# A three-layer decoder block on one core: third buffers for two tiles, a 128x128 turn, and new orders on all five engines

## What is computed

```python
# layer 1: recurrent attention, 32 heads of 16, mixed with the row before
xx = shifted(x) - x
r, k, v, g = ((x + xx * maa_i) @ Wi.T + bi for each i)     # four projections
y = (r @ k * Wm) @ v                                        # decay and bonus in Wm
y = (head_norm(y) * ln_g + ln_b) * silu(g);  x = x + y @ Wo.T + bo
# layer 2: attention over ctx_512, 32 query heads, 8 key/value heads
x = x + softmax(q @ k / 4) @ v
# layer 3: MLP; inputs of both products are quantised in blocks of 32 to 8 bits
h = mx_linear(mx_layernorm(x), W1, b1);  h = mx_gelu(h)
x = x + bf16_round(residual + mx_linear(h, W2, b2))
```

## Time and profile before

| | |
|---|---|
| median of 3 runs | 1352.62 us |
| lowest and highest | 1351.16, 1355.15 us |
| span of the profiled execution, first to last instruction | 1347.5 us |
| PE busy | 1243.7 us, 92% |
| DVE busy | 1137.6 us, 84% |
| ACT busy | 797.9 us, 59% |
| POOL busy | 660.0 us, 49% |
| chain that ended last | PE 52%, DVE 20%, issue 10%, ACT 6%, POOL 6%, DMA 4% |

### The profile page before, as it was taken

One profiled execution on the slowest core, in us unless ns is written; L12 is line 12 of the kernel. 1 busy time (PEld: TensorE's weight loads), 2 busy tenths in 40 slices (PEclk: granted clock), 3 DMA queues, 4 the chain that ended last, 5 costly groups with the idle time before them and its releaser, 6 DMA issues.

```text
span 1347.5 us, 34631 instructions
## 1 busy us (share of the span) xinstructions
PE 1243.7 (92%) x13352; PEld 795.7 (59%) x13352; DVE 1137.6 (84%) x1960; ACT 797.9 (59%) x1565; POOL 660.0 (49%) x700
## 2 busy tenths in 40 slices
PE   4778999999999999999999999999999999999864
PEld 4556556666665556666555666655566666566421
DVE  7899888888888888888888888888888898889885
ACT  3334657566666675666667665566666665675541
POOL 6767354555454444544444454544445444445332
PEclk9889999999999999999999999999999999999987
DMA  7664332222233222122322212223122322222222
GB/s 240 165 152 118 83 81 54 55 60 57 63 67 70 71 49 54 52 62 67 71 71 49 55 51 59 71 70 70 38 53 60 65 71 70 51 59 57 60 57 51
DMA packets 137331, 97.09 MB, mean 72 GB/s; under 512 B 108112, under 2 KB 110160, under 8 KB 136400
## 3 DMA queue, kind: packets, MB, share of 16 engines
q1 hardware_dynamic: 137168, 94.87, 27.9%
HBM read 37.16 MB, written 8.39 MB: 34 GB/s over the span
## 4 chain that ended last, share of the span: by engine, by line
PE 52%; DVE 20%; issue 10%; ACT 6%; POOL 6%; DMA 4%; SPq 1%; ACTq 0%; POOLq 0%; DVEq 0%
PE bank_b L549 12%; PE bank_y L603 7%; PE bank_a L549 7%; PE bank_a L539 5%; PE rt L618 3%; PE rt L631 3%; PE rt L568 2%; DVE att L1430 2%; DVE negm L1459 2%; DVE amax_g L1500 2%; PE bank_a L658 2%; PE bank_o L595 2%; PE bank_b L658 2%; PE bank_o L637 2%; DMA xin<-x 2%
## 5 line engine op out<-in xcount | busy, mean ns | idle before, releaser
L3011 POOL TENSOR_TENSOR gmem<-gmem,unit_g 128x1024 bf16<-128x1024 bf16 x64 | 125.9, 1968 | 250.8 <-DVE unit_g L1512 250.8
L1459 DVE TENSOR_REDUCE negm<-rt 128x16 f32<-128x2048 f32 x64 | 145.9, 2280 | 3.1 <-PE rt L618 2.8
L2433 ACT ACTIVATE pT<-rt 128x2048 f32<-128x2048 f32 x64 | 119.9, 1873 | 23.3 <-PE rt L631 17.3
L667 PE MATMUL bank_y<-w2q,gmem 128*128 128x512 bf16 x512 | 120.6, 387 | 8.3 <-DMA gmem<-gmem 8.3
L549 PE MATMUL bank_a<-mix_r,w_Wr 128*128 128x128 f32 x1024 | 125.2, 282 | 0.9 <-POOL mix_r L2970 0.9
L549 PEld LDWEIGHTS bank_a<-mix_r,w_Wr 128*128 128x128 f32 x1024 | 120.5, 197 | 7.8 <-issue 7.7
L549 PEld LDWEIGHTS bank_b<-mix_k,w_Wk 128*128 128x128 f32 x1024 | 118.3, 193 | 5.2 <-issue 3.8
L549 PE MATMUL bank_b<-mix_g,w_Wg 128*128 128x128 f32 x1024 | 120.4, 276 | 1.1 <-POOL mix_g L2970 1.0
L549 PE MATMUL bank_b<-mix_k,w_Wk 128*128 128x128 f32 x1024 | 119.8, 275 | 1.3 <-DMA w_Wk<-Wk 1.2
L603 PE MATMUL bank_y<-w_Wo,yT 128*128 128x512 f32 x256 | 116.3, 597 | 3.7 <-issue 2.2
L549 PEld LDWEIGHTS bank_b<-mix_g,w_Wg 128*128 128x128 f32 x1024 | 116.8, 192 | 4.0 <-issue 3.2
(11 more groups left out here) (185 smaller groups left out, 2814.1 us busy)
## 6 DMA issues: line engine op xcount, KB each, us to landing
qx<-qdense SPq DMA_DIRECT2D x64, 224.0 KB, 3.0
context<-ctx SPq DMA_DIRECT2D x32, 384.0 KB, 3.2
gmem<-w SPq DMA_DIRECT2D x16, 512.0 KB, 4.1
xin<-x SPq DMA_DIRECT2D x32, 256.0 KB, 3.3
out<-x SPq DMA_DIRECT2D x32, 256.0 KB, 3.0
vp<-vz SPq DMA_DIRECT2D x32, 128.0 KB, 3.1
odense<-oT SPq DMA_DIRECT2D x128, 32.0 KB, 1.9
pT<-Wv SPq DMA_DIRECT2D x1, 1024.0 KB, 8.9
```

The costliest lines, as they stand in the source:

```text
L667: done = e.matmul(bank_y[:, :], gqT[:, t, :], w2q[:, t, :], start=(t == 0), stop=(t == FT - 1))
L1459: e.tensor_reduce(negm[:, 0:H].rearrange("p (g a j) -> p g j a", g=4, a=2)[:, :, 2 * i:2 * i + 2, :], rt[:, :].rearrange("p (g j a s) -> p ...
L2433: e.activation(pT[:, :, :].rearrange("p g n -> p (g n)"), rt[:, :], ACT.Exp, scale=float(D) ** -0.5).then_inc(sem(f"act_ex{i}"), 1)
L3011: e.tensor_tensor(blocks(half), blocks(half), per_block(unit[f"g{i}"], 32), ALU.mult).then_inc(sem(f"pool_gsc{i}"), 1)
```

## The change

xin and x2 get a third buffer each, and the semaphores that count their loads and stores become three. `next_x(n)` waits for `first_sum` of n - 3 rather than n - 2, and `normalise_o(n)` for the store of n - 3. oden becomes [128, 128], set to zero once on POOL, and `turn_sums` transposes all of it. Every other step computes what it did; each engine has the same steps as before, 866 on PE, 1414 on DVE, 1084 on ACT, 339 on POOL and 398 on SP, in another order. The loops are shorter: `range(13, 25)` on PE, `range(14, 24)` on DVE, `range(13, 25)` on ACT, `range(14, 25)` on POOL, `range(17, 24)` on SP; the turns around them are written out singly. Waits in the lists that an earlier wait already covers are left out.

```diff
-        xin = [sb(f"xin{i}", [P, C]) for i in range(2)]
+        xin = [sb(f"xin{i}", [P, C]) for i in range(3)]
...
-        oden = sb("oden", [H, T])
+        oden = sb("oden", [P, T])
...
-        x2 = [sb(f"x2_{i}", [P, C]) for i in range(2)]
+        x2 = [sb(f"x2_{i}", [P, C]) for i in range(3)]
...
             def next_x(n):
-                if n >= 2:
-                    e.wait_ge(sem("dve_x1"), n - 1)
-                    load_x(n)
+                if n >= 3:
+                    e.wait_ge(sem("dve_x1"), n - 2)
+                load_x(n)
...
             def turn_sums(n):
...
-                e.transpose(bank_o[:, 0:H], oden[:, :], ident[0:H, 0:H]).then_inc(sem("pe_dT"), 1)
+                e.transpose(bank_o[:, 0:P], oden[:, :], ident[:, :]).then_inc(sem("pe_dT"), 1)
...
             def normalise_o(n):
...
-                if n >= 2:
-                    e.wait_ge(sem(f"sp_out{n % 2}"), 16 * (n // 2))
+                if n >= 3:
+                    e.wait_ge(sem(f"sp_out{n % 3}"), 16 * (n // 3))
...
             load("masks")
+            load_w12(0)
             load("columns")
             load("heads")
-            load_w12(0)
             load_x(0)
             load_w12(1)
+            load("Wv")
+            load("Wk")
             load_x(1)
-            load("Wv")
             load("Wr")
```

More of the change, by code:

```diff
@@ L1793, in _ @@
             norm_mv("g", 2)
+            mixed(5, "k")
+            gate(4)
             weighted(2)
+            stats_q(6)
             hidden(2)
@@ L1923, in _ @@
             hidden(5)
-            mixed(8, "v")
+            gelu_max(4, 1)
             hidden_max(5)
@@ new lines, in _ @@
+            up_out(6, 0, bank_a)
+            first_sum(8)
+            stats_x(8)
+            gelu_max(6, 0)
+            gelu_pow2(6, 0)
+            norm_mv("x", 8)
+            decayed(9, 0)
+            up_out(6, 3, bank_b)
+            denominators(7)
+            second_out(5)
+            residual(5)
+            differences(10)
+            mixed(10, "v")
+            maxima(8, 1)
+            normalise_o(7)
+            gelu_round(6, 0)
+            up_out(6, 2, bank_a)
+            stats_f(7)
@@ new lines, in _ @@
+            mixed(10, "k")
+            maxima(8, 0)
+            gate(9)
+            norm_mv("f", 7)
+            decayed(9, 1)
+            stats_g(7)
+            norm_mv("g", 7)
+            gelu_max(6, 1)
+            weighted(7)
+            hidden(7)
+            hidden_max(7)
+            gelu_pow2(6, 1)
+            hidden_pow2(7)
+            hidden_scale(7)
+            gelu_quantised(6, 0)
+            hidden_round(7)
+            hidden_quantised(7)
+            scaled_y(9)
+            stats_q(11)
@@ new lines, in _ @@
+            maxima(9, 1)
+            up_out(7, 2, bank_a)
+            gelu_quantised(7, 0)
+            mixed(11, "v")
+            mixed(11, "k")
+            normalise_o(8)
+            residual(6)
+            maxima(9, 0)
+            stats_f(8)
+            norm_mv("f", 8)
+            gate(10)
+            decayed(10, 1)
+            stats_g(8)
+            norm_mv("g", 8)
+            weighted(8)
+            hidden(8)
+            hidden_max(8)
+            gelu_max(7, 1)
+            hidden_pow2(8)
@@ new lines, in _ @@
+            decayed(11, 0)
+            gelu_pow2(8, 0)
+            denominators(9)
+            second_out(7)
+            residual(7)
+            up_out(8, 2, bank_a)
+            differences(12)
+            normalise_o(9)
+            maxima(10, 1)
+            mixed(12, "v")
+            mixed(12, "k")
+            maxima(10, 0)
+            stats_f(9)
+            norm_mv("f", 9)
+            gelu_round(8, 0)
+            gelu_max(8, 1)
+            gate(11)
+            gelu_quantised(8, 0)
@@ new lines, in _ @@
+            stats_q(13)
+            norm_mv("q", 13)
+            first_sum(11)
+            stats_x(11)
+            norm_mv("x", 11)
+            decayed(12, 0)
+            gelu_max(9, 0)
+            gelu_pow2(9, 0)
+            up_out(9, 3, bank_b)
+            denominators(10)
+            differences(13)
+            maxima(11, 1)
+            normalise_o(10)
+            second_out(8)
+            up_out(9, 2, bank_a)
+            mixed(13, "v")
+            maxima(11, 0)
+            stats_f(10)
@@ L1966, in _ @@
[L1966 to L1976 removed]
+            decayed(22, 1)
+            stats_g(20)
+            norm_mv("g", 20)
+            weighted(20)
+            hidden(20)
@@ new lines, in _ @@
+            normalise_o(22)
+            up_out(21, 2, bank_a)
+            maxima(23, 1)
+            mixed(25, "v")
+            maxima(23, 0)
+            stats_f(22)
+            mixed(25, "k")
+            norm_mv("f", 22)
+            gelu_round(21, 0)
+            gate(24)
+            gelu_quantised(21, 0)
+            stats_g(22)
+            decayed(24, 1)
+            norm_mv("g", 22)
+            weighted(22)
+            hidden(22)
+            hidden_max(22)
+            hidden_pow2(22)
```

2424 lines of the change are left out of this document (1739 added, 685 removed).

## The result

The changed kernel takes 1376.64 us (1375.84 to 1377.2) beside 1352.59 for the kernel of before in the same comparison: a ratio of 1.0174, interval 1.015 to 1.0198. The forecast was 1333, its range 1322 to 1349, and slower had the chance 0.08. The span went from 1347.5 to 1374.0 us, at a mean granted clock of 0.978.

What follows compares the result with a forecast made beforehand. PE was taken to bound the middle, with only its idle time to lose: -27.3 idle, +7.7 overlaps in the loop, +3.3 other turns, -3 start, 0 end, together -19.3 us, from 1352.6 to 1333.3; range 1322 to 1349.

Steps and rivals of the forecast that it cites:

- Third buffers: In the middle: DVE's 19.9 us of waits for the store go, and PE's 8.8 us on the hidden rows, too.
- a sign of being wrong: In the middle: the forecast is wrong if PE keeps a wait on `hqT` or `xq`.
- Worth by themselves: nothing but what PE gets out of it: Third xin and x2: by themselves they bring only what reaches PE, counted within its idle time.
- The loop: Eleven turns: `mixed` beside POOL loses 1.9 us, 1.2 to spare, so PE stalls 0.7 a turn, 7.7 us.
- Rivals A: Loop: the overlaps of `mixed` with POOL cost nothing; -27 us, 1326; chance 0.25.
- B: Loop: POOL's multiplications lock DVE, too; stall 1.85 us a turn, 1346; chance 0.2 together with a rival of useless buffers.
- Other turns: Thirteen singly written turns between 150 and 1100 us: 0.25 us each, 3.3 us (1.5 to 8).
- Start: Up to `decayed(0, 0)`: `distances(0)` fills DVE's idle time, w12 is requested earlier, PE gains the same: -3 us (-6 to +3).
- the risk that the forecast had named with its order of loads: Start: Wo ahead of a piece of w12 and Wr after Wk may delay DVE and cost as much as the gain.
- End: From `project("g", 31)` on: orders nearly the same, PE's 37.8 us idle stay; 0 (-2 to +2).
- turn_sums as 128x128: On PE: the larger transpose costs 0 to 0.09 us each, 0 to 2.9 in all; taken as 0.
- Rival C: Loop: DVE becomes the bound ahead of `scores_r`; stall 2.5 us in 14 turns, 35 us, 1361; chance 0.1.

Runs made afterwards that it cites:

- e9: Kernel of before with a third buffer of x2 and nothing else: 1339.71 us, ratio 0.9904.
- e1: Kernel of before in its orders, with third buffers of xin and x2 and the 128x128 turn of the sums: 1339.41 us, ratio 0.9899.
- e6: Changed kernel with POOL's operations on two tensors replaced by memsets that read nothing: 1324.03 us, ratio 0.9798.
- its control: Orders of before with third buffers and 128x128 turn, POOL's operations on two tensors replaced by memsets: 1335.04 us, ratio 0.9877.
- e2: Changed kernel with the orders of before up to the output turn of turn 8: 1355.09 us, ratio 1.0022.
- e8: Old orders, third buffers, 128x128 turn; DVE's statistics of x ahead of decayed 0, x loaded one place earlier on SP: 1327.86 us, ratio 0.9819.

## Why the prediction was wrong, by its steps

Between forecast (-19.3 us) and the measured spans (+26.5) lie 45.8 us: 12.4 of them in the start, 21.9 from turn 3 to 27, 11.5 at the end.

*Third buffers: right, and undersold.* DVE's wait for the store went as said, and in the loop so did PE's on `hqT`. Outside it 6.0 us of that wait are left between 320 and 1060; the forecast had all 8.8 gone, and named such a wait as a sign of being wrong. And the step "Worth by themselves: nothing but what PE gets out of it" left out that the old orders get it, too. e9 has 12.6 us of gain from one tile, of the 27.3 of idle time. The forecast booked the whole 27.3 us to buffers and orders together and never asked what the orders add.

*The loop: the overlap right, the gain undersized.* The stall at `scores_r` was forecast at 0.7 us a turn and is 0.61. The gain by the sum was 27.3 / 24 - 0.7, some 0.4 us a turn; turns 14 to 24 won 0.97 each. These ten had more idle time than the average that was booked, 14.2 us before and 6.0 after. And the gain is not the orders': e1 has the same 38.6 us a turn. Rivals A and B are out for the loop: mixes of 2.11 and 1.91 us are not 1.13, and the stall is not B's 1.85.

*"Other turns: I give them 0.25 us each", 3.3 us in all: the step that failed most.* From turn 3 to 27 I had forecast -16.3 us; it was +5.6 (947.4 us for 941.8): +13.0 from turn 3 to 8, +1.5 to turn 14, -9.7 to turn 24, +0.8 to turn 27. I took the singly written turns for copies of a good one with a little more friction. They are other orders, in which the pair of `mixed` and a reading POOL step occurs again and again, two POOL steps at a time. The earlier trace rows showed the price, 3.72 us for four, the one group of before that took over 3 us; the changed kernel has at least five (3.44, 4.42, 3.16, 4.79 and 3.67 us, at 30, 253, 372, 1164 and 1247). I used the price for a rival in the loop and did not look in the new orders for where else the pair stands. e6, in which POOL's steps on two tensors read nothing, takes 917.9 us from turn 3 to 27 instead of 947.4, and its control 930.5.

*Start: -3 forecast, +9.4 measured by turn 3.* "Up to `decayed(0, 0)` DVE has the same steps as before, so PE gains what DVE gains" fails at once. DVE comes to `decayed(0, 0)` later than before (46.76 after 44.40), not earlier, and PE waits until 48.58 rather than 46.22:

```profile
29.54 3.44 DVE L1865 SCALAR_TENSOR_TENSOR mix_v<-xx,all_columns,xT 128x128 f32<-128x128 f32 x4
...
43.25 1.22 DVE L2044 TENSOR_REDUCE amax_w<-gmem 128x32 f32<-128x1024 f32 x1 [1.03 <-DMA gmem<-w]
...
46.76 1.76 DVE L1890 TENSOR_TENSOR att<-rt,wm 128x1536 f32<-128x1536 f32 x1
...
48.58 1.14 PE L689 MATMUL rt<-rz,kT 32*64 32x192 f32 x48 [3.09 <-DVE att L1890]
```

The gain of the first step never came: `distances(0)` could start only at 6.55, behind ACT's `per_head`, and the first w12 step stands at 8.23 rather than 7.93. `mixed("v")` took 3.44 us instead of 1.58, and 1.03 us went to a wait for a piece of w12 that before had come in time, the risk that the forecast had named with its order of loads. POOL's `bonuses` is not the difference: a piece of w12 takes 3.66 us beside it, but before `differences` stood there and took 2.80 instead of 0.68, and in e6, where `bonuses` still reads and a piece takes 3.83, turn 3 comes at 164.9. How much of the 9.4 us is which is open; e1, with the order of before, has turn 3 at 172.5, 3.3 us later than before. By turn 8 it is 22.4 us. e2 gave back 21.5.

*End: 0 (-2 to +2) forecast, +11.5 measured.* "From `project("g", 31)` on the orders are nearly the same" was true and beside the point, for the loss begins at turn 27, which the sum put among the 0.25 us turns. The prediction named this as what would make it wrong.

*turn_sums as 128x128: nothing against it.* It takes 0.27 us instead of 0.24, within the 0 to 0.09 forecast, and e1, which has it and a third xin, is not slower than e9, which has neither. It was not run alone.

*Rival C had the sign and the mechanism, and the wrong place.* It put DVE's lateness in the loop at `scores_r`, 35 us. It came in the turns around the loop, at `project("k")` and `values_r` behind a late `mixed("k")` or `decayed`, and in places the slow clock, which the forecast had priced nowhere, added to it. I held it at 0.1 because in the loop `gate_parts` comes after `maxima(n-2, 0)`; in turns 8 and 28 it stands right at the mixes.

What stays open: how much of the loss is the clock's, and why 2 us of idle time brought a slow clock at one place and not at two others. At turn 8 it is 1.70 us, but no run separated the idle from the slow matmuls behind it. Nor was a kernel tried that keeps the new start and end and only parts the mixes from POOL's readers there.

## What to carry to other kernels

When an order is laid out anew, list on every in-order engine which instruction now stands beside which on the others, in the singly written turns as well as in the loop: a VectorE step with two SBUF inputs beside a GpSimd step on two tensors cost most of the overlap here (2.03 us of 2.5, 1.64 of 2.1), one beside multiplications by a column only 0.35 us, and the nearest row of the old trace gives the price. Before crediting an order with a gain, ask what the buffers alone bring to the old order; here one more tile gave 12.6 us and the move of three steps some 11 more (e8 against e1), while the new orders with a POOL that only writes gave 11. After a stall of two or three microseconds on TensorE look at the granted clock and the length of the step behind it; here some of these stalls cost 1.70 us more, and some nothing.

## What the runs showed of the hardware that I had not expected

- Whether POOL reads decides between two orders by 48 us in 1350: the same two sets of orders differ by +37.2 us with a reading POOL and by -11.0 with a writing one.
- The four instructions of a `mixed` beside four POOL operations in a row took 4.79 us instead of 1.13.
- Idle times of 0.94 and 1.98 us, 1.4 us apart, were followed by a `project("k")` of 5.44 us instead of 3.74, at a mean granted clock of 0.69 from 380 to 384. One of 2.07 us was followed by one of 3.81 us at a clock of 1.00, and the waits of 0.6 us a turn in the loop left the clock at 1.00.
- DVE's wait for a store, 1.1 us a turn on an engine that is busy 84% of the time, cost PE 0.9 us a turn (39.6 before, 38.6 with the third x2 alone).
